# Turning four of ten units of attention probabilities by DMA instead of on TensorE, with a longer lead

## The reference, cut to what matters

```python
x = x + 0.5 * ffn(layernorm(x))
x = x + attention(layernorm(x))
x = x + 0.5 * ffn(layernorm(x))

def attention(x):
    latents = x @ W_down.T
    q = x @ W_q.T
    k, v = latents @ W_uk.T, latents @ W_uv.T
    scores = einsum('bhqd,bhkd->bhqk', q, k) / sqrt(128)
    attn = softmax(where(causal, scores, -inf))
    return (attn @ v) @ W_o.T
```

## Time and profile before

| | us |
|---|---|
| median of 3 runs | 251.86 |
| range of the runs | 251.26 to 251.86 |
| the profiled execution | 251.87 |
| its span (first to last instruction) | 249.9 |
| TensorE, VectorE, ScalarE, GpSimd busy | 237.5, 206.2, 163.6, 71.9 |
| attention, from the first score product to the start of the projections | 64.51 to 196.58 |

### The profile page before, as it was taken

The page is one execution under the profiler, slowest core; times in us unless marked ns, Lnnn a source line. Parts: engine busy times, 40 slices in busy tenths (PEclk is TensorE's granted clock), DMA queues, the critical chain, the costliest instruction groups (busy, mean ns, idle before and its releaser), DMA issues.

```text
span 249.9 us, 7272 instructions
## 1 busy us (share of the span) xinstructions
PE 237.5 (95%) x2643; PEld 182.1 (73%) x2668; DVE 206.2 (82%) x487; ACT 163.6 (65%) x320; POOL 71.9 (29%) x127
## 2 busy tenths in 40 slices
PE   7789999999789999999999999999998899999995
PEld 2545479966667868879788787787887788855474
DVE  2978799895879989999999899999999518268793
ACT  2646581485878887978888798888889500335560
POOL 8320234000003434524354334344455000210230
PEclk9999999999999999999999999999999999999999
DMA  6999400001102014216034160251427330000005
GB/s 223 236 312 352 89 4 0 3 0 45 42 3 67 21 31 95 43 46 122 10 76 81 42 125 1 70 100 32 96 41 87 24 63 3 0 0 3 0 1 168
DMA packets 34792, 17.21 MB, mean 69 GB/s; under 512 B 25484, under 2 KB 34520, under 8 KB 34520
## 3 DMA queue, kind: packets, MB, share of 16 engines
q1 hardware_dynamic: 33576, 15.81, 27.6%
q10 hardware_dynamic: 1200, 1.18, 1.4%
HBM read 7.55 MB, written 1.05 MB: 34 GB/s over the span
## 4 chain that ended last, share of the span: by engine, by line
PE 77%; DVE 16%; issue 3%; DMA 1%; ACT 1%; DVEq 0%
PE bank L1088 12%; PE bank L901 10%; PE bank L852 9%; PE bank L1163 8%; PE bank L1079 7%; PE bank L1008 6%; PE bank L1078 4%; PE bank L1102 3%; PE bank L1101 3%; PE bank L1103 3%; PE bank L1035 3%; PE bank L1080 2%; DVE pT_lo L756 2%; DVE nmax L751 2%; DVE nmax L747 2%
## 5 line engine op out<-in xcount | busy, mean ns | idle before, releaser
L506 ACT ACTIVATE prob<-bank,nmax 128x384 f32<-128x384 f32 (+3 forms) x128 | 62.3, 528 | 8.2 <-DVE nmax L747 6.8
L756 DVE TENSOR_TENSOR pT_lo<-bank,pT_hi 128x512 f16<-128x512 f32 x80 | 54.6, 684 | 3.1 <-ACT pT_hi L512 2.4
L512 ACT CAST pT_hi<-bank 128x512 f16<-128x512 f32 x80 | 46.8, 585 | 11.1 <-PE bank L1088 10.6
L1088 PE MATMUL bank<-ident,prob 128*128 128x128 f32 x320 | 50.5, 280 | 0.2 <-ACT prob L506 0.2
L387 POOL TENSOR_TENSOR cst<-craw,rsum 128x256 f32<-128x256 f32 x30 | 18.4, 614 | 93.2 <-DVE craw L765 93.2
L1101 PE MATMUL bank<-lat,pT_hi 128*128 128x65 bf16 x320 | 37.7, 193 | 2.3 <-DVE pT_lo L756 2.3
L1102 PE MATMUL bank<-lat,pT_hi 128*128 128x64 bf16 x320 | 37.8, 195 | 0.0
L1079 PE MATMUL bank<-latT_lo,wqo 128*128 128x384 bf16 (+3 forms) x128 | 36.6, 299 | 1.2
L1103 PE MATMUL bank<-lat,pT_lo 128*128 128x65 bf16 x320 | 37.5, 192 | 0.0
L1101 PEld LDWEIGHTS bank<-lat,pT_hi 128*128 128x128 f16 x320 | 30.1, 96 | 7.2 <-DVE pT_lo L756 2.0
L747 DVE TENSOR_REDUCE nmax<-bank 128x1 f32<-128x512 f32 (+1 forms) x48 | 32.8, 682 | 2.1 <-PE bank L1080 2.1
(11 more groups left out here) (173 smaller groups left out, 463.5 us busy)
## 6 DMA issues: line engine op xcount, KB each, us to landing
wqo<-stage SPq DMA_DIRECT2D x64, 64.0 KB, 2.0
wqo<-in_L_attn_W_q_dram SPq DMA_DIRECT2D x1, 2048.0 KB, 9.5
wqo<-in_L_attn_W_o_dram SPq DMA_DIRECT2D x1, 2048.0 KB, 15.6
out_dram<-X SPq DMA_DIRECT2D x8, 128.0 KB, 1.8
X<-in_L_attn_x_dram ACTq DMA_DIRECT2D x1, 512.0 KB, 7.1
cT<-in_L_attn_W_uk_dram SPq DMA_DIRECT2D x1, 512.0 KB, 11.2
cT<-in_L_attn_W_uv_dram SPq DMA_DIRECT2D x1, 512.0 KB, 11.0
cT<-in_L_ffn_w_dram SPq DMA_DIRECT2D x1, 384.0 KB, 4.8
```

The source lines that it names most:

```text
L506: last = nc.scalar.activation(prob[:, u % 2, cols], bank[SCORE_BANK[u]][:, cols], ACT.Exp, bias=nmax[:, u, n:n + 1])
L512: nc.scalar.copy(pT_hi[:, j % 2, :], bank[3 + j % 2][:, :]).then_inc(pThi_ready, 1)
L756: nc.vector.tensor_tensor(pT_lo[:, j % 2, :], bank[3 + j % 2][:, :], pT_hi[:, j % 2, :], ALU.subtract).then_inc(pTlo_ready, 1)
L1088: last = nc.tensor.transpose(bank[3 + j % 2][:, blk(k)], prob[:, j % 2, blk(k)], ident[:, :])
```

## The change

Units 1, 3, 6 and 8 of a pair (`BY_DMA`) are no longer turned on TensorE. ScalarE copies their probabilities to a 16-bit high part in SBUF (`high_part`), GpSimd subtracts it to make the low part (`low_part`), and SP turns both parts with one DMA transpose of eight blocks (`turn_probabilities`) into one of two buffers `turned`, which `context` reads. The other six units (`BY_PE`) go the old way, and their transposes are now issued two such units ahead (`second_next`).

Scores run 7 units ahead instead of 4 (`LEAD`), with 5 buffers of probabilities; bank 7 serves unit 0 and the queries. On VectorE the maximum comes first in a step, then the low part, then, one step later than before, the copy of the context. The query chunks stand at the end of steps 4 and 6 on TensorE, for the pair after next; the queries of pair 1 are made ahead of the loop. SP moves both chunks at once with four DMAs of twice the width, and turns both parts of a pair's contexts with one DMA.

```diff
+    SCORE_BANK = [7, 0, 1, 2, 0, 1, 2, 0, 1, 2]
+    HELD_BY = [None, -3, -2, -1, 1, 2, 3, 4, 5, 6]
+    LEAD = 7
+    BY_DMA = [1, 3, 6, 8]
+    BY_PE = [u for u in range(UNITS) if u not in BY_DMA]
+    PROBS = 5
...
 SP:
+            def move_queries(i):
+                sp.wait_ge(u_lo, i * 2 + 2)
+                for side in range(2):
+                    for part in range(2):
+                        sp.dma_start(uc[LAT * part:LAT * (part + 1), i * 2 + side:i * 2 + side + 1, :],
+                                     stage[LAT * side:LAT * (side + 1), part:part + 1, :]).then_inc(u_moved, 16)
+            def turn_probabilities(i, j):
+                d = in_order(BY_DMA, i, j)
+                sp.wait_ge(prob_lo, d + 1)
+                if d >= 2:
+                    sp.wait_ge(turned_used, d - 1)
+                sp.dma_start_transpose(turned[:, d % 2, :, :].rearrange("p a (k q) -> p (a k) q", k=SB),
+                                       prob_hl[:, d % 2, :, :].rearrange("p a n -> p (a n)")).then_inc(prob_turned[d % 2], 16)
...
             for i in range(NP):
+                turn_probabilities(i, 6)
+                turn_probabilities(i, 8)
+                if i > 0:
+                    sp.wait_ge(clo_ready, B + 2 * B * i)
+                    sp.dma_start_transpose(cT[:, i - 1, :, :, :].rearrange("p a n t -> p (a n) t"),
...
+                if i < NP - 1:
+                    turn_probabilities(i + 1, 1)
+                if i < NP - 2:
+                    move_queries(i + 2)
+                if i < NP - 1:
+                    turn_probabilities(i + 1, 3)
...
 GpSimd:
+            def low_part(i, j):
...
+                nc.gpsimd.tensor_tensor(prob_hl[:, r, 1, :], prob[:, j % PROBS, :], prob_hl[:, r, 0, :],
+                                        ALU.subtract).then_inc(prob_lo, 1)
...
+                low_part(i, 8)
+                divide_context(i, 0, 0)
+                low_part(i, UNITS + 1)
+                divide_context(i, 0, 1)
+                low_part(i, UNITS + 3)
+                divide_context(i, 1, 0)
+                low_part(i, UNITS + 6)
+                divide_context(i, 1, 1)
...
 ScalarE:
+            def high_part(i, j):
...
+                nc.scalar.copy(prob_hl[:, d % 2, 0, :], prob[:, j % PROBS, :]).then_inc(prob_hi, 1)
...
             def attention_step(i, j, queries=True):
-                if not beyond(i, j + 3):
-                    exponent(i, j + 3)
-                if queries and j in (1, 3):
-                    split_queries(i + 1, j // 2)
-                if not beyond(i, j + 2):
-                    split(i, j + 2)
+                if not beyond(i, j + LEAD - 1):
+                    exponent(i, j + LEAD - 1)
+                if j % UNITS in BY_PE:
+                    if not beyond(i, second_next(j)):
+                        split(i, second_next(j))
+                elif not beyond(i, j + HU):
+                    high_part(i, j + HU)
+                if queries and j in (5, 7):
+                    split_queries(i + 2, (j - 5) // 2)
...
 VectorE:
             def attention_step(i, j, queries=True):
-                side, unit = divmod(j - 1, HU)
-                if j and unit in LAST_UNIT:
+                side, unit = divmod(j - 2, HU)
+                if not beyond(i, j + LEAD):
+                    row_max(i, j + LEAD)
+                if j > 0 and (j - 1) % UNITS in BY_PE and not beyond(i, second_next(j - 1)):
+                    split(i, second_next(j - 1))
+                if j > 1 and unit in LAST_UNIT:
                     take_context(i, side, LAST_UNIT.index(unit))
-                if not beyond(i, j + 1):
-                    split(i, j + 1)
-                if not beyond(i, j + 4):
-                    row_max(i, j + 4)
-                if queries and j in (1, 3):
-                    split_queries(i + 1, j // 2)
+                if queries and j in (5, 7):
+                    split_queries(i + 2, (j - 5) // 2)
...
 TensorE:
             def attention_step(i, j, with_queries=True):
-                if with_queries and j in (1, 3):
-                    queries(i + 1, j // 2)
-                if not beyond(i, j + 4):
-                    scores(i, j + 4)
+                if not beyond(i, j + LEAD):
+                    scores(i, j + LEAD)
                 context(i, j)
-                if not beyond(i, j + 2):
-                    transposes(i, j + 2)
+                if j % UNITS in BY_PE and not beyond(i, second_next(j)):
+                    transposes(i, second_next(j))
+                if with_queries and j in (4, 6):
+                    queries(i + 2, (j - 4) // 2)
...
+            for t in range(2):
+                queries(1, t)
             pe.wait_ge(lat_lo, 3)
```

More of the change, by code:

```diff
@@ L231, in bass_macaron_moe_mla_moe @@
         u_lo = sem("u_lo")
-        u_moved = [sem(f"u_moved{t}") for t in range(2)]
+        u_moved = sem("u_moved")
         s_ps = sem("s_ps")
@@ L235, in bass_macaron_moe_mla_moe @@
         prob_ready = sem("prob_ready")
+        prob_hi = sem("prob_hi")
+        prob_lo = sem("prob_lo")
+        prob_turned = [sem(f"prob_turned{r}") for r in range(2)]
+        turned_used = sem("turned_used")
         pT_ps = sem("pT_ps")
@@ L272, in blk, with second_next, in_order @@
             return slice(n * P, (n + 1) * P)
+        def second_next(j):
+            n = BY_PE.index(j % UNITS) + 2
+            return j - j % UNITS + n // NPE * UNITS + BY_PE[n % NPE]
+        def in_order(units, i, j):
+            assert j % UNITS in units
+            return i * len(units) + (j // UNITS * len(units) + units.index(j % UNITS))
         def beyond(i, j):
@@ L294, in _ @@
             sp.wait_ge(woT_hi, 8)
[L295 to L298, removed]
-            for i in range(NP):
[L301 to L309, removed]
@@ new lines, in _ @@
+            for j in (1, 3, 6):
+                low_part(0, j)
+            with pool.Fori(0, NP - 1) as i:
+                low_part(i, 8)
[6 more added lines that the diff above has]
+                divide_context(i, 1, 1)
+            low_part(NP - 1, 8)
+            for b in range(B):
+                divide_context(NP - 1, 0, b)
@@ L1083, in transposes @@
             def transposes(i, j):
+                n = in_order(BY_PE, i, j)
+                r = BY_PE.index(j % UNITS) % 2
                 pe.wait_ge(prob_ready, i * UNITS + (j + 1))
-                if not (isinstance(i, int) and i == 0 and j < 2):
-                    pe.wait_ge(pTlo_ready, i * UNITS + (j - 1))
+                if not (isinstance(i, int) and n < 2):
+                    pe.wait_ge(pTlo_ready, n - 1)
                 for k in range(SB):
-                    last = nc.tensor.transpose(bank[3 + j % 2][:, blk(k)], prob[:, j % 2, blk(k)], ident[:, :])
+                    last = nc.tensor.transpose(bank[3 + r][:, blk(k)], prob[:, j % PROBS, blk(k)], ident[:, :])
                 last.then_inc(pT_ps, 1)
             def context(i, j):
-                unit = j % HU
+                unit, u = j % HU, j % UNITS
                 if unit == 0 or unit == 2:
                     pe.wait_ge(ctx_free, i * (2 * B) + (j // HU * B + unit // 2 + 1))
-                pe.wait_ge(pTlo_ready, i * UNITS + (j + 1))
+                if u in BY_DMA:
+                    d = BY_DMA.index(u)
+                    pe.wait_ge(prob_turned[d % 2], i * (8 * ND) + 16 * ((j // UNITS * ND + d) // 2 + 1))
+                    parts = [turned[:, d % 2, part, :] for part in range(2)]
+                else:
+                    pe.wait_ge(pTlo_ready, in_order(BY_PE, i, j) + 1)
+                    parts = [p[:, BY_PE.index(u) % 2, :] for p in (pT_hi, pT_lo)]
                 for b, q, at in HEAD_UNITS[unit]:
@@ L1103, in context @@
                         last = mm(dst, p_lo, lat[:, n, 0:LAT + 1], start=False, stop=(k == q))
+                if u in BY_DMA:
+                    last.then_inc(turned_used, 1)
                 if unit in LAST_UNIT:
```

168 lines of the change are left out of this document (102 added, 66 removed).

## The result

The changed kernel takes **278.35 us** (median of five runs, 275.71 to 279.78) where the kernel before takes 251.86 (five runs, 251.26 to 252.23): the ratio is 1.104 with a 95% interval of 1.101 to 1.108. The forecast was 262.5 with a range of 254 to 268, so the sign was right, and the loss was 26.5 us instead of 10.6.

What follows compares the result with a forecast made beforehand. TensorE bounds the loop at 16.2 us per pair; the change makes it 14.64 of work plus waits of 1.14 and 1.18, 16.96. With a longer fill and end waits, projections start 10.6 us later: 262.5 us, range 254 to 268.

Steps and rivals of the forecast that it cites:

- Wait 1: Loop, step 6: TensorE waits 1.14 us before the second query chunk until VectorE's low half of the first frees bank 7.
- the fill: Ahead of the loop: pair 1's queries delay the first score product to 70.95 and the first context to 80.5.
- wait 2: Loop: TensorE waits 1.18 us for the next pair's unit 3, whose DMA turn stands behind four moves in SP's queue.
- 14.64 + 1.14 + 1.18 = 16.96 us: Loop period per pair: TensorE's work plus the two waits, 0.76 us more than the kernel before.
- landing of 3.3 us: DMA turns: time from issue start to landing, taken from today's context transposes, which take 2.4 to 4.4.
- second rival: DMA turns land early, in 2.4 us, giving 254.4 us; chance 0.17.
- third's: Third rival: DMA turns land in 4.4 us, as the late ones do, giving 272.4 us; chance 0.08.
- the forecast's own signs of being wrong: Period under 16.2, TensorE transposes in every step, first context before 76, or loop waits released by GpSimd or ScalarE.
- The sum: Whole kernel: projections start at 207.2 instead of 196.58, 10.6 us later, then both kernels do the same.
- 5.3 us of waiting for turns: End of the loop: the last pair's turned units 3, 6 and 8 hold TensorE up by 1.5 + 1.3 + 2.5 us.
- TensorE stays the bound: Rival: no waits in the loop or at the end, 9.3 us faster than now, 242.6 us; chance 0.12.
- SP's issue time is hidden: Rival: unit 3's turn leaves when its low part is ready, its wait is 0.5 us, total 258.4; chance 0.08.

Runs made afterwards that it cites:

- e1: The changed kernel with VectorE's copy of the context back at the head of its step, one step earlier: 268.20 us.
- e2: The changed kernel with ScalarE copying the query chunk ahead of the cast of its step: 267.43 us.
- e3: The changed kernel with the edits of e1 and e2 together: 258.31 us, ratio 1.026 to the kernel before.
- e8: e3 plus e5's fill, SP's first two turns ahead of the second pair's moves, and loop query chunks behind the scores of steps 5 and 7: 254.65 us.
- e11: e9 without its two edits of the fill, so with the fill of the change: 250.40 us, ratio 0.994 to the kernel before.
- e10: e9 with SP's fill order moves, turn 1, moves, turn 3, and ScalarE copying the second chunk ahead of unit 3's cast: 249.55 us.
- e5: The changed kernel with the second pair's query chunks put between the first scores in the fill, not ahead of them: 279.34 us.
- e9: e8 with units 6 and 8 of the last pair turned on TensorE: 251.76 us.

## Why the prediction was wrong

**What held.** The sign and its kind: waits that hang on the order inside one queue, where TensorE stops being the bound. Wait 1 was put at 1.14 us from start to start and costs 1.13, with VectorE's stage as its releaser as foretold. The first score product came at 71.70 (70.95), the first context at 81.37 (80.5), the loop's first chunk at 87.45 (by the same count 86.7): the fill was 0.75 too short. The turn of unit 3 leaves 4.5 us after the end of step 7, as counted (4.57): the moves do stand ahead of it, and at twice the width they hold SP for 2.38 us, unchanged from 2.39, as assumed. That the loop came out slower is luck in part: without wait 2, which did not show, the forecast's own pair is 15.78 us, under today's 16.2. At 0.4 us per pair such a loop would not have won back the fill, which brings the first context 10.9 us later, so the sign of the whole is not luck.

**The step that failed** is "So a pair takes 14.64 + 1.14 + 1.18 = 16.96 us". It takes these two waits for all there are. The edit that moves `take_context` a step later and behind the maximum and the low part was given no cost and no cover. The trace of the kernel before could have given it, as VectorE's timeline there has the same instructions:

```profile
123.52 0.69 DVE L756 TENSOR_TENSOR pT_lo<-bank,pT_hi 128x512 f16<-128x512 f32 x1
124.12 0.68 DVE L747 TENSOR_REDUCE nmax<-bank 128x1 f32<-128x512 f32 x1
124.72 0.17 DVE L764 RECIPROCAL rsum<-bank 128x4 f32<-128x4 f32 x1
124.81 0.39 DVE L765 COPY craw<-bank 128x256 f32<-128x256 f32 x1
```

In the forecast's own count, from the end of step 7, VectorE begins the low half of chunk 1 at 1.43. Behind it stand, from start to start, that low half (0.61), a maximum of two parts (0.66), a low part (0.60), a maximum (0.60), the reciprocal (0.09) and the copy of 0.39, so the copy ends at 4.38. TensorE wants the bank after steps 8 and 9 and one score product, 0.99 + 1.38 + 0.60 = 2.97. That is a wait of 1.41 before any hand-over; measured 1.60 from start to start. The other wait, 1.22, follows from the order alone. The copy stands behind the maximum of the scores of one step before, and from the start of that maximum it takes 1.88 us until the context starts (138.54 to 140.42), where TensorE has some 0.7 left to do (until 139.20). e1 took both out, and with them 1.51 of the pair's excess; e2 and e3 showed the rest.

**Terms of the wrong size.** Wait 2 rested on a landing of 3.3 us, from the transposes of contexts; turns land in 2.8 (2.7 to 4.7 in the whole run), between the second rival's 2.4 and the third's 4.4. With 2.8 it would have been 4.5 + 2.8 - 6.72 = 0.6, and the missed waits covered that. A wait of 0.37 for ScalarE's exponentials ahead of the first chunk was counted once for the fill and belongs to each pair; a releaser on ScalarE in the loop was among the forecast's own signs of being wrong. TensorE's work was put at 14.64 us per pair and is 14.38, since the earlier trace rows were read by the starts of loads: a set of transposes takes 0.47 from start to start and not 0.39, so the change takes 1.88 off TensorE and not 1.56.

**The sum.** The projections were put at 207.2 and started at 220.63, 13.4 later: 0.75 from the fill, 5 x (18.87 - 16.96) = 9.55 from the loop, and 3.1 that are left over for the end. There the forecast had 5.3 us of waiting for turns, and 1.8 shows; the copies, which it did not have, are waited for 6.9 from 181.78 on. The median lies 2.6 us above the profiled execution.

**The rivals.** "TensorE stays the bound" asked that no waits be left, and put the kernel at 242.6. In e8 to e11 the loop runs about 0.4 us per pair above TensorE's work, and the kernel comes to 249.55 at best; the difference lies mostly in the fill and the end, where its subtraction took away all waiting, and the fill of e10 still waits 1.97 for a turn. "SP's issue time is hidden" falls as well: in the change the turn of unit 3 has its low part at 136.16 and leaves at 137.06, 0.10 us after the moves' 2.38 us of issue end, and in e5 the first turn 0.04 after 2.39. The Trainium skill (DMA: Bandwidth & Descriptors, section Issuing engines are not separate DMA queues) says that issue time is usually small against the DMA itself. Here it is not: a group of four issues takes 2.4 us and a turn behind it lands in 2.8.

## What to carry to other kernels

When a change moves an instruction inside an engine's queue, price it like a new wait: take the time at which it now ends, from the rows of all that stands ahead of it, and the time at which the engine that needs its buffer gets there. A release that stands behind work on what the consumer made a step ago cannot come early, however idle the engine is: here it cost 1.22 us per pair. And a gain ahead of an in-order queue is only had if everything in that queue moves with it: the fill's 3.9 us went from one wait to the next.

## What was not expected of the hardware

**The granted clock** is 1.00 throughout in the profiles of the kernel before and of the change, but in other executions it falls for some microseconds in the fill and ahead of the projections, after stretches in which TensorE had little to do. Busy time by stretch, first of the change, then of e3 (us, PE, PEld, DVE, ACT, POOL, clock, DMA share, GB/s):

```profile
64.00:68.00 4.00, 2.07 (x20) 0.90 (x14) 2.24 (x5) 1.76 (x3) 0.00 (x0) 1.00 0.43 100
68.00:72.00 4.00, 1.77 (x8) 0.73 (x9) 1.31 (x2) 1.74 (x2) 0.00 (x0) 1.00 0.00 0
```

```profile
64.00:68.00 4.00, 1.91 (x16) 0.74 (x12) 2.41 (x5) 1.66 (x3) 0.00 (x0) 1.00 0.42 99
68.00:72.00 4.00, 2.11 (x8) 0.73 (x9) 0.98 (x2) 1.81 (x2) 0.00 (x0) 0.68 0.00 0
72.00:76.00 4.00, 4.00 (x21) 2.71 (x20) 2.14 (x4) 1.11 (x4) 0.00 (x0) 0.50 0.56 131
```

0.50 is the lower of the two levels, 1.2 GHz, and the same score product of 512 columns takes 0.63 us there and 0.38 at the higher. Much the same work (2.07 and 1.91 us busy of 4 in the stretch ahead) went on at full clock in one execution and not in the other, so what decides it stays open. The times go with it: in the 14 runs of e9, those at a clock of 1.000 took 248.12 to 249.32, the one at 0.966 took 256.87.

**The width of a move** does not show in its issue time: four moves of 128 KB hold SP for 2.38 to 2.40 us here, and four of 64 KB held it for 2.39 in the kernel before. They land in 2.3 us instead of 2.0.
